# A graph network layer with residual and LayerNorm on one core: the load of x moved behind the sources, the end of the last step rearranged, and a short last output round

## What is computed

```python
def ref(node_inputs, edge_inputs, src, dst, W, b, eps):
    msg = jax.nn.relu(node_inputs[src] + edge_inputs)
    agg = jax.ops.segment_sum(msg, dst, num_segments=12500)
    h = (1.0 + eps[0]) * node_inputs + agg
    return h @ W.T + b
x = _layernorm(x + ref(x, edge_attr_32, src, dst, W, b, eps), axis=-1)
```

## Time and profile before

| what | value |
|---|---|
| time, median of 3 runs | 2145.62 us (2144.47 to 2146.45) |
| the profiled execution | 2143.99 us, of which its span is 2142.2 us |
| TensorE busy | 2036.5 us, 95% of the span |
| VectorE busy | 1680.4 us, 78% |
| ScalarE busy | 1725.3 us, 81% |
| GpSimd busy | 1550.7 us, 72% |
| chain of work that ended last | TensorE 93%, VectorE 3%, issue 2%, DMA 1% |
| first matmul | at 7.20 us |
| first product of the output (L1215) | at 2112.44 us |

### The profile page before, as it was taken

One profiled execution on the slowest core, in us unless ns is written; L12 is line 12 of the kernel. 1 busy time (PEld: TensorE's weight loads), 2 busy tenths in 40 slices (PEclk: granted clock), 3 DMA queues, 4 the chain that ended last, 5 costly groups with the idle time before them and its releaser, 6 DMA issues.

```text
span 2142.2 us, 126630 instructions
## 1 busy us (share of the span) xinstructions
PE 2036.5 (95%) x49720; PEld 1933.2 (90%) x49720; DVE 1680.4 (78%) x4603; ACT 1725.3 (81%) x1833; POOL 1550.7 (72%) x1570
## 2 busy tenths in 40 slices
PE   2899999999999999999999999999999999999995
PEld 1799999999999999999999999999999999999991
DVE  6878877777778888777777787888787777787874
ACT  4688888888888888888888888888888888888872
POOL 5377777777777777777777777777777777777760
PEclk9999999999999999999999999999999999999997
DMA  5465555656655555655555555555655555565541
GB/s 125 93 117 114 114 117 118 117 117 117 118 113 114 116 117 113 115 118 117 117 118 116 115 113 116 115 116 113 118 117 117 117 117 116 113 115 116 115 95 31
DMA packets 261593, 241.87 MB, mean 113 GB/s; under 512 B 115281, under 2 KB 232187, under 8 KB 261568
## 3 DMA queue, kind: packets, MB, share of 16 engines
q1 hardware_dynamic: 207944, 212.61, 47.9%
q0 software_dynamic: 50048, 25.72, 8.6%
q10 hardware_dynamic: 3576, 3.20, 0.5%
HBM read 238.52 MB, written 2.81 MB: 113 GB/s over the span
## 4 chain that ended last, share of the span: by engine, by line
PE 93%; DVE 3%; issue 2%; DMA 1%; ACT 0%; DVEq 0%; SPq 0%; ACTq 0%
PE found L1117 52%; PE l L1097 22%; PE win L1128 10%; PE ranks L1160 3%; PE ranks L1151 3%; PE ranks L1149 1%; PE l L1215 1%; DMA oh<-in_src 1%; DMA slots<-slot_dram 0%; PE l L1201 0%; DMA slot_dram<-slot_row 0%; PE found L1045 0%; DVE xparts L601 0%; DVE rows_all L731 0%; DVE oh L598 0%
## 5 line engine op out<-in xcount | busy, mean ns | idle before, releaser
L498 POOL DMA_INDIRECT rows_all<-in_x,index x1564 | 1550.2, 991 | 526.4 <-issue 477.7
L1117 PE MATMUL found<-table,oh 128*128 128x128 bf16 x18732 | 1180.5, 220 | 27.9 <-DVE oh L716 1.5
L1117 PEld LDWEIGHTS found<-table,oh 128*128 128x128 bf16 x18732 | 1095.1, 132 | 64.6 <-ACT table L918 50.1
L1097 PE MATMUL l<-xparts,oh 128*57 128x96 bf16 x21408 | 498.1, 207 | 1.8 <-issue 1.0
L1097 PEld LDWEIGHTS l<-xparts,oh 128*57 128x57 bf16 x21408 | 467.6, 108 | 17.8 <-issue 2.2
L943 ACT ACTIVATE oh<-slots,minus_lanes 128x1824 bf16<-128x1824 f16 x223 | 402.9, 1807 | 14.8 <-DMA slots<-slot_dram 12.9
L918 ACT CAST table<-l 128x768 bf16<-128x768 f32 x446 | 356.3, 799 | 62.8 <-PE l L1097 25.3
L950 ACT ACTIVATE oh<-oh 128x1824 bf16<-128x1824 bf16 x223 | 384.5, 1724 | 0.0
L962 ACT ACTIVATE oh<-keys,minus_lanes 128x896 bf16<-128x896 f16 x223 | 232.4, 1042 | 178.7 <-PE found L1117 178.7
L731 DVE COPY_PREDICATED rows_all<-mask,found 128x224 f32<-128x224 uint16 x892 | 358.8, 402 | 11.2 <-PE found L1117 4.2
L704 DVE TENSOR_SCALAR oh<-slots,lanes 128x1824 bf16<-128x1824 f16 x446 | 288.4, 688 | 2.3 <-DMA slots<-slot_dram 2.3
(11 more groups left out here) (124 smaller groups left out, 924.6 us busy)
## 6 DMA issues: line engine op xcount, KB each, us to landing
slots<-slot_dram SPq DMA_DIRECT2D x223, 456.0 KB
msg<-in_edge SPq DMA_DIRECT2D x446, 112.0 KB
keys<-key_dram SPq DMA_DIRECT2D x223, 224.0 KB
rows_all<-in_x,index POOLq DMA_INDIRECT x1564
index<-in_src SPq DMA_DIRECT2D x223, 3.5 KB
key_dram<-key SPq DMA_DIRECT2D x223, 1.8 KB
slot_dram<-slot_row SPq DMA_DIRECT2D x223, 3.6 KB
dst_rows<-in_x ACTq DMA_DIRECT2D x1, 1562.5 KB
```

Source lines behind the costliest of these rows:

```text
L498: pool.indirect_dma_start(to, None, x, bass.IndirectOffsetOnAxis(indices[:, j:j + 1], 0)).then_inc(done, 16)
L1097: last = nc.tensor.matmul(l1_of(g)[half * HALF:half * HALF + CAP, :, :], oh1[:, j, b * CAP:(b + 1) * CAP], xparts[:, j * EVEN + b, :, :], ...
L1117: last = nc.tensor.matmul(found[:, t * FOUND:(t + 1) * FOUND], marks[:, t, :], table[:, b, n * FOUND:(n + 1) * FOUND],  start=(b == 0 and ...
```

## The change

- **Start.** The three loads of x and the two of its remainder move from ScalarE's queue to SP's, behind the two loads of the sources and ahead of the index, dst and weight loads. VectorE waits for the first half of the sources alone. The second half is transposed into `found` and copied to `src_sb` by ScalarE, ahead of its first `round_x`.
- **describe.** `place` and `side` become int32 and are written by one instruction each, so that two copies go from each of its four calls. Both are read once in every step: `place` by L683, `side` by L725.
- **Last step.** `find_far` runs in step 222, with one reduction of `rel` (read as unsigned bits) in place of two, and makes `bad` there. The product of the flag and the first four x terms (L1201, `begin_output`) go behind the sum of step 223 on TensorE; VectorE copies the flag in step 223.
- **Rounds.** `ROUNDS_OUT` becomes 1, 4, 4, 4, 4, 4, 3, 1 tiles: eight rounds. `turn_x` uses the same list.

```diff
-    ROUNDS_OUT = [(0, NT % OGROUP)] + [(t, OGROUP) for t in range(NT % OGROUP, NT, OGROUP)]
+    ROUNDS_OUT = [(0, 1)] + [(t, min(OGROUP, NT - 1 - t)) for t in range(1, NT - 1, OGROUP)] + [(NT - 1, 1)]
...
-        place = sb("place", [P, LOOK, ROWS], F16)
+        place = sb("place", [P, LOOK, ROWS], I32)
...
-        side = sb("side", [P, LOOK, ROWS], F16)
+        side = sb("side", [P, LOOK, ROWS], I32)
...
+            for j in range(SUBS):
+                sp.dma_start(x_stage[:, j * EVEN:(j + 1) * EVEN, :]..., x_even[j]).then_inc(stage_loaded[j], 16)
+            sp.wait_ge(stage_cleared, 1)
...
-                own(nc.vector.tensor_scalar(t, n, EVEN.bit_length() - 1, None, ALU.logical_shift_right))
-                nc.vector.tensor_copy(place[:, :, some], t)
+                own(nc.vector.tensor_scalar(place[:, :, some], n, EVEN.bit_length() - 1, None, ALU.logical_shift_right))
...
-                own(nc.vector.tensor_scalar(t, n, SIDE - 1, None, ALU.bitwise_and))
-                own(nc.vector.tensor_copy(side[:, :, some], t))
+                own(nc.vector.tensor_scalar(side[:, :, some], n, SIDE - 1, None, ALU.bitwise_and))
...
-            dve.wait_ge(sources_turned, 2)
+            dve.wait_ge(sources_turned, 1)
...
-                nc.vector.tensor_reduce(rel_max[:, :], rel[:, :, :], AX.XY, ALU.max)
-                nc.vector.tensor_reduce(rel_min[:, :], rel[:, :, :], AX.XY, ALU.min)
+                nc.vector.tensor_reduce(rel_max[:, :], rel[:, :, :].bitcast(U16), AX.XY, ALU.max)
...
+            def flag_far():
+                dve.wait_ge(bad_summed, 1)
+                nc.vector.tensor_copy(far_flag[:, :], ranks[0:1, 0:1]).then_inc(flag_ready, 1)
...
+                    if st.s == ROWS - 1:
+                        find_far()
                     if st.s == ROWS:
-                        find_far()
+                        flag_far()
...
+            act.wait_ge(sources_turned, 2)
+            for k in range(2):
+                tiles, turned = turned_late(k)
+                last = nc.scalar.copy(src_sb[:, tiles.start:tiles.stop, P:ROWS], turned)
+            last.then_inc(late_taken, 1)
             round_x(0, x_high)
...
+                if not st.inside and st.s == ROWS:
+                    sum_bad()
+                    begin_output()
```

More of the change, by code:

```diff
@@ L381, in turned_sources, with turned_late @@
             return l1[k][:, :].rearrange("p (t b) -> p t b", t=2)
+        def turned_late(k):
+            tiles = range(LOOK)[k * LATE_TILES:(k + 1) * LATE_TILES]
+            return tiles, found[:, k * 512:k * 512 + len(tiles) * (ROWS - P)].rearrange("p (t b) -> p t b", b=ROWS - P)
         def turned_nodes(k):
@@ L803, in step @@
                     if st.s == FROM + 1:
-                        take_sources(slice(EARLY, ROWS)).then_inc(sources_taken, 1)
+                        take_sources(slice(EARLY, P)).then_inc(sources_taken, 1)
                         dve.wait_ge(sources_taken, 1)
@@ L870, in _ @@
         def _(act):
[L871 to L876, removed]
             def clear_sums(k):
@@ L1029, in _, with turn_sources @@
             pe.wait_ge(ones_ready, 1)
[L1030 to L1035, removed]
+            def turn_sources(h, to, t):
+                b0, b1 = HALF_ROWS[h][1:]
+                return nc.tensor.transpose(to, src_f[0:b1 - b0, h, :].rearrange("b (p t) -> b t p", t=LOOK)[:, t, :], ident[0:b1 - b0, 0:b1 - b0])
+            pe.wait_ge(sources_cast, 1)
+            for t in range(LOOK):
+                last = turn_sources(0, turned_sources(t // 2)[:, t % 2, 0:P], t)
+            last.then_inc(sources_turned, 1)
+            pe.wait_ge(sources_cast, 2)
+            for k in range(2):
+                tiles, to = turned_late(k)
+                for t in tiles:
+                    last = turn_sources(1, to[:, t - tiles.start, :], t)
+            last.then_inc(sources_turned, 1)
             def turn_x(st):
@@ L1161, in fill_slots, with x_term, begin_output, sum_bad @@
                     last.then_inc(slots_ready, 1)
+            def x_term(k):
+                t0, per = ROUNDS_OUT[k]
+                nc.tensor.matmul(zT[k % ZRING][:, 0:per * NP], wx[:, :], x_turned[:, t0:t0 + per, :], start=True, stop=False, skip_group_check=True)
+            def begin_output():
+                pe.wait_ge(table_ready, ROWS * 2)
+                for k in range(ZRING):
+                    x_term(k)
+            def sum_bad():
+                pe.wait_ge(bad_ready, 1)
+                nc.tensor.matmul(ranks[0:1, 0:1], bad[:, :], one_col[:, :], start=True, stop=True).then_inc(bad_summed, 1)
             def step(st):
@@ L1181, in _ @@
             steps(pe, step, 1)
-            pe.wait_ge(bad_ready, 1)
-            nc.tensor.matmul(ranks[0:1, 0:1], bad[:, :], one_col[:, :], start=True, stop=True).then_inc(bad_summed, 1)
             pe.wait_ge(flag_ready, 1)
@@ L1197, in _ @@
                     sum_far(row + 1, TILES)
-            def x_term(k):
-                t0, per = ROUNDS_OUT[k]
-                nc.tensor.matmul(zT[k % ZRING][:, 0:per * NP], wx[:, :], x_turned[:, t0:t0 + per, :], start=True, stop=False, skip_group_check=True)
-            pe.wait_ge(table_ready, ROWS * 2)
-            for k in range(ZRING):
-                x_term(k)
             pe.wait_ge(agg_ready, 1)
```

23 lines of the change are left out of this document (15 added, 8 removed).

## The result

The changed kernel takes **2121.52 us** (median of 4 runs, 2118.97 to 2123.52), the kernel before beside it 2146.03 (4 runs, 2144.47 to 2149.46): ratio 0.9883, interval 0.9866 to 0.99. The forecast was 2122.0, and 2120.4 for the profiled execution. The profiled executions are 2123.52 us after (span 2121.7) and 2143.99 before; the one after is the slowest of its four, so the profiles differ by 20.5 us where the medians differ by 24.5.

A forecast was written before the change was run, and what follows sets the result against it. TensorE, busy 95% of the span, was taken as the bound, so only start and end could move: 2143.99 - 11.8 - 11.1 - 0.7 = 2120.4 us profiled, 2122.0 for the median; range 2115 to 2130.

The forecast's parts named there:

- The first half's landing: Start: the sources' first half lands and is cast at 4.9 us (bounds 4.3 and 6.1), VectorE starts about 7.85.
- The second half's landing: Start: the sources' second half lands at about 7.5 us, needed by 8.7, with 0.1 us lost at row 0.
- The split: Start: VectorE's two-pass split of x ends at 24.5 us in place of 33.16, 8.65 us earlier.
- describe: Two copies fewer save 1.74 us per call; two calls on VectorE's chain before the turn of x give -3.5 us.
- The turn of x: TensorE's turn of x starts near 63.2 us in place of 75.25; the start sums to -11.8 us (-8 to -15).
- The end: After TensorE's last look-up: earlier `find_far` and x terms give -11.1 us (-9.2 to -13.3), first pick 2.55 us late.
- The output: Last output rounds: the short round starts the last three stores about 0.85 us earlier, giving -0.7 us (-0.2 to -0.9).
- x comes late: Rival, start: x behind the sources in one queue arrives late, 3.7 us lost, 2125.7 us; chance 0.10.
- The loop gets longer: Rival, loop: int32 reads lengthen the mask beyond 0.44 us of slack; chance 0.02 slower, 0.02 about no change.
- The start's gain is taken back: Rival, steps 0 to 2: row 1's DMAs meet x's output load, at most 3.5 us lost, 2125.5 us; chance 0.10.
- The clock stays at half: Rival, last sums, x terms and first rounds at half clock: +2.0 and up to 1.9 us, 2125.9; chance 0.08.
- Reordering does nothing: Rival, end: only the dropped reduction counts, -3.3 us in place of -11.1, 2129.8 us; chance 0.03.

The follow-up runs named there:

- e6: The changed kernel with x loaded from ScalarE's queue again: 2125.57 us, ratio 0.9903, 5.4 us slower than e5.
- e10: The kernel before with int32 `place` and `side` alone, on a usual chip: 2146.32 us, ratio 0.9981.
- e12: e8 plus 34 products, results unread, ahead of TensorE's first look-up: 2124.66 us, ratio 0.9885 to the kernel before.
- e4: The kernel before with the eight output rounds alone, on the slow chip: 3010.80 us, ratio 1.0004.
- e8: The changed kernel with unread products filling TensorE's waits in step 223 and for the flag: 2118.19 us, ratio 0.9866 to the kernel before.
- e3: The kernel before with the change of the last steps alone, on the slow chip: 3000.52 us, ratio 0.9963.
- e5: The changed kernel measured again, unaltered: 2120.15 us against 2146.55 for the kernel before, ratio 0.9873.
- e7: The changed kernel with the seven old output rounds: 2120.96 us, ratio 0.988 to the kernel before.
- e11: The kernel before with the change of the last steps alone, on a usual chip: 2142.22 us, ratio 0.9958.
- e9: The kernel before with the start's change alone, on a usual chip: 2142.63 us, ratio 0.9966.
- e1: The kernel before with the start's change alone, on the slow chip: 3016.97 us against 3011.43, ratio 1.0018.

## Why the prediction was right, and where it was not

- **The first half's landing: right.** Cast at 4.62 (4.9 said), VectorE at 7.56 (7.85 said). e6 shows that the queue does it: with x on ScalarE's queue the cast is at 6.03.
- **The second half's landing: mis-sized.** "I expect about 7.5", and it was about 9.1; the limit I had worked out was 8.7. In the other six profiles with x behind the sources this half is cast at 8.10 to 9.23, so 7.5 was too early in all of them. So the "0.1 us lost" at row 0's ranks was 0.9 (the wait of 1.97, where before had 1.09). The prediction gives no working for the 7.5. The Trainium skill, DMA: Bandwidth & Descriptors (Why a DMA increments its semaphore by 16 and not by 1), makes 95 rows go over five engines, and I used that in a rival only. The late landing is what this rule would lead one to expect, but no run tells it from x's packets beside it.
- **The split: right in sum.** -8.24 (-8.65 said). The thin cover of ScalarE's copies held: its middle parts came at 18.92 (18.8 said).
- **describe: right.** 0.46 us each, 1.79 per chunk (1.74 said), -3.7 alone in e10 (-3.5 said), in a stage that scatters by 1.5 where nothing was changed.
- **The turn of x: right.** 63.78 (63.2 said), the first look-up -12.16 (-11.8 said). Between the split's end and the turn it took 37.6 to 40.3 us in six profiles of the changed kernel and its variants (42.1 before), with the half clock at a different place each time. e12, warmed up, has the 37.6, 1.1 to 2.7 us less than the other five.
- **The end: right within its range,** -12.1 (-11.1 said, -9.2 to -13.3). First pick 2.80 us late (2.55 said), x terms 3.73 between my 2.75 and 5.50: half clock first, the return within them, as said.
- **The output: the step that failed.** I said -0.7 and got +1.5. The short round itself does what I said (-0.6 in e4, and in every profile at full clock), though the reading under it was loose: in the earlier trace rows the steady rate of the end carries some 0.6 MB, a little over two stores of 256 KB and not three. What I left out of the sum, and priced as a rival at 8 in 100, is that the clock falls again after the x terms: TensorE had idled 4.29 us ahead of the sum and 1.61 ahead of the first product, and the half clock then ran from about 2092.4 to 2102.7, which cost 2.1 us (beside e8). In before, the wait lay ahead of the x terms and they took the half clock on themselves. With them in the last step, part of the half clock fell behind them in five of six profiles (after, e3, e5, e7, e11; not in e6). That the waits bring it is shown by e8, where both are filled and the clock stays full; what decides how much of it reaches the output is not shown.
- **The rivals.** "x comes late": refuted, VectorE never waits for x, and e6 has x at its old queue and is slower. "The loop gets longer": the mask takes 192 ns and not 188, far from the 0.44 us of slack. "The start's gain is taken back": refuted on the usual chips (e9); in e1 the gain was gone at the turn of x, but behind TensorE's gaps with no releaser and not behind a DMA. "The clock stays at half": true in part, and worth 0 to 2.1 us in the output. "Reordering does nothing": refuted by e3 and e11.

That the median came out 0.5 us from the forecast is in part luck. Errors of both signs met: 1.0 more gained at the end and 0.4 at the start, against 2.2 less in the output. The profiled execution, for which 2120.4 was forecast, took 3.1 us longer: these 0.8, and 2.3 of a longer loop, which is within the loop's scatter. That the median has less of it was not forecast.

## What to carry to other kernels

Where a first instruction waits for a load, look at what else is in flight at that time: here putting another engine's 1.5 MB behind the sources in one queue was worth 3.7 to 4.7 us of the start, about as much as splitting the wait. At an end where TensorE waits for short reductions, run them a step earlier, then ask where the waits that remain put the half clock, since it costs whatever comes next; filling both such waits with products that nobody reads paid 2.0 us here (e8). When parts of a change are measured alone, compare stages of the trace too: this loop of 2000 us scatters by 12 us between profiles, as much as the largest part gives.

## What was not expected of the hardware

- **Some matmuls do not follow the clock.** Eight products of `aggX` (fp32, read with a step of four elements) take 1.96 us at half clock (2096.31 in after) and 1.94 at full (2092.36 in e8), while the transposes between them go from 1.22 to 0.70. Four of them at a time write different rows of the result and overlap (one takes 1055 ns on average in after, 1049 in e8, and eight end within 1.96). What limits them instead no run shows.
- **What else is issued decides when a load lands.** 448 KB were there for a cast at 4.62 with x behind them in one queue, and at 6.03 with x issued by a second engine at the same time.
- **One chip of those used is slower for TensorE.** The kernel before takes 3011 us on it instead of 2146. It was not profiled there; e1, on that chip, has 353 us of "issue" ahead of the look-up's products, where before has 1 us on another chip. Why is not shown.
